# GNN megakernel on one core: the setup around a power on GpSimd, with operands and results moved to PSUM, the power cut in two, and the step masks made later

## What is computed

```python
def reference(x, src, dst, edge_attr, edge_weight, edge_weight1, ...):
    h = layernorm_relu(x)                                   # "norm_x"
    ew = concat([edge_weight, ones(N)])                     # edges and loops
    deg = segment_sum(ew, dst_and_loops, N)
    dis = where(deg > 0, rsqrt(deg), 0)
    for W, b in ((W0, b0), (W1, b1), (W2, b2)):             # three GCN layers
        h = relu(segment_sum((h @ W)[src] * dis[src] * ew * dis[dst], dst) + b)
    ...                                                     # a GIN layer: segment_sum(ew * x[src])
    att = edge_weight1 ** lam                               # the power; used only in the attention
    ...                                                     # attention over the edges: segment softmax, masks by node
    ...                                                     # a SAGE layer: a mean over the in-edges
```

## Time and profile before

| | us |
|---|---|
| median of 3 runs | 6796.12 |
| the profiled execution | 6801.79 |
| its span | 6800.1 |
| GpSimd busy, of the span | 4779.3 (70%) |
| VectorE busy | 3946.1 (58%) |
| TensorE busy | 4822.0 (71%) |
| ScalarE busy | 1132.7 (17%) |
| first gather of pass 0 starts | 305.0 |

### The profile page before, as it was taken

One profiled execution on the slowest core, in us unless ns is written; L12 is line 12 of the kernel. 1 busy time (PEld: TensorE's weight loads), 2 busy tenths in 40 slices (PEclk: granted clock), 3 DMA queues, 4 the chain that ended last, 5 costly groups with the idle time before them and its releaser, 6 DMA issues.

```text
span 6800.1 us, 95655 instructions
## 1 busy us (share of the span) xinstructions
PE 4822.0 (71%) x25896; PEld 3192.9 (47%) x25896; DVE 3946.1 (58%) x11854; ACT 1132.7 (17%) x2990; POOL 4779.3 (70%) x4783
## 2 busy tenths in 40 slices
PE   0367667677767677777577777699999974777775
PEld 0244444444444444444344444566666653444444
DVE  8744555544555545555544444588888886444445
ACT  0200000100000100000100000377777763000000
POOL 6377777777777677777677777477777742777773
PEclk9788998888898888888788888899999987888887
DMA  2122222222222222222222222366666641222221
GB/s 56 47 53 53 53 54 53 72 53 53 53 53 53 67 53 53 53 53 53 61 53 53 53 53 53 82 141 143 142 146 140 142 94 32 53 53 53 53 53 47
DMA packets 384863, 466.43 MB, mean 69 GB/s; under 512 B 103802, under 2 KB 290616, under 8 KB 384326
## 3 DMA queue, kind: packets, MB, share of 16 engines
q0 software_dynamic: 152528, 313.83, 18.6%
q1 hardware_dynamic: 201066, 129.25, 8.4%
q10 hardware_dynamic: 30748, 17.23, 0.9%
HBM read 434.51 MB, written 27.81 MB: 68 GB/s over the span
## 4 chain that ended last, share of the span: by engine, by line
POOL 46%; issue 19%; PE 13%; DVE 10%; DMA 9%; SPq 2%; ACT 1%; DVEq 1%; ACTq 0%; POOLq 0%
POOL pool L710 45%; DMA pool<-table,src_col 4%; DMA pool<-edge_attr 3%; DVE work L1538 2%; PE psum L896 2%; PE psum L887 2%; PE psum L880 2%; PE psum L850 2%; PE psum L922 1%; DMA gath<-table,src_col 1%; DVE pool L1380 1%; PE psum L824 1%; SPq L611 1%; PE psum L848 1%; PE psum L866 1%
## 5 line engine op out<-in xcount | busy, mean ns | idle before, releaser
L710 POOL DMA_INDIRECT pool<-table,src_col x3910 | 3701.1, 947 | 1467.1 <-issue 1143.8
L850 PE MATMUL psum<-pool 128*128 x8300 | 1924.0, 321 | 1413.0 <-DVE pool L1546 1409.7
L850 PEld LDWEIGHTS psum<-pool 128*128 128x128 f32 x8300 | 1695.8, 220 | 2556.1 <-issue 2231.9
L848 PE MATMUL psum<-busy_rows,iota_b 128*128 128x512 bf16 x7820 | 2694.1, 431 | 72.3 <-issue 72.1
L1546 DVE TENSOR_SCALAR pool<-iota_f,rel_col,ew_col 128x128 f32<-128x128 f32 x3320 | 1225.3, 370 | 1803.7 <-SPq L492 1789.2
L690 POOL DMA_INDIRECT gath<-table,src_col x832 | 904.6, 1087 | 281.4 <-issue 223.9
L1538 DVE SCALAR_TENSOR_TENSOR work<-psum,dis,work 128x128 f32 x2490 | 870.9, 350 | 144.2 <-PE psum L850 112.8
L848 PEld LDWEIGHTS psum<-busy_rows,iota_b 128*128 128x128 bf16 x7820 | 847.6, 110 | 181.7 <-issue 95.9
L1546 DVE TENSOR_SCALAR pool<-iota_f,rel_col 128x128 f32<-128x128 f32 x830 | 267.6, 323 | 436.8 <-SPq L492 433.3
L1081 ACT ACTIVATE pool<-psum 128x512 f32<-128x512 f32 (+1 forms) x104 | 58.1, 565 | 1989.4 <-PE psum L812 1989.4
L1538 DVE SCALAR_TENSOR_TENSOR work<-psum,inv_cnt,work 128x128 f32 x830 | 291.4, 351 | 106.2 <-PE psum L850 76.9
(11 more groups left out here) (212 smaller groups left out, 3767.9 us busy)
## 6 DMA issues: line engine op xcount, KB each, us to landing
pool<-table,src_col POOLq DMA_INDIRECT x3910
pool<-edge_attr SPq DMA_DIRECT2D x832, 64.0 KB
pool<-step_masks SPq DMA_DIRECT2D x624, 48.0 KB
pool<-rel_rows SPq DMA_DIRECT2D x208, 128.0 KB
gath<-table,src_col POOLq DMA_INDIRECT x832
table<-work ACTq DMA_DIRECT2D x48, 256.0 KB, 2.3
table<-QV SPq DMA_DIRECT2D x12, 256.0 KB, 2.3
table<-work SPq DMA_DIRECT2D x12, 256.0 KB, 2.3
```

What stands on the lines that cost most here:

```text
L710: gp.indirect_dma_start(out=gath_ring[:, t % RING, :], out_offset=None, in_=source[:, :], in_offset=bass.IndirectOffsetOnAxis(ap=src_col[: ...
L848: pe.matmul(psum[:, SUM_BANKS, :], iota_b[:, :], busy_rows[:, :], start=True, stop=True)
L850: pe.matmul(psum[:, steps.bank(s), 0:D], hot_ring[:, s % HOT_RING, :], gath_ring[:, bass.ds(slots[s % REGS], 1), :].rearrange("p a d -> p ...
```

## The change

1. **The power.** `lam` and the distances are loaded first of all, on ScalarE's queue (they were late on ScalarE's and SyncE's). VectorE makes `lam_row` ahead of the plan. GpSimd computes the first 100 of 800 elements (`FIRST_POW`) before the seven indirect DMAs and the other 700 right behind them, without the wait for `norm_x.shift`.
2. **PSUM operands.** The ones exist in SBUF and in PSUM (`ones_col`, `ones_ps`), and an instruction takes the one on the other side of its tensor. Destinations (`dst_ps`), digits, `block2`, `rstd_ps`, the low digit (`low_ps`) and the weights (`ew_ps`, the transposed weights left in their banks) are in PSUM. `tile_src` is cast in two halves of 7 x 64, in place, straight. The low digit's instructions are halved.
3. **The right-hand side of the degrees** is made by four instructions per chunk, one for each digit, instead of from a one-hot `low_hot` made ahead.
4. **Order.** Only six of the ten blocks of columns (destinations, weights, sources) are turned before the degrees. All the rest of the masks, with the other four, is `masks_vector`, behind the last `gcn_drain(0)`. ScalarE stores the rows of each group as before, but scales `AGG` for all 13 groups only after `masks_made`. The waits of the gathers for `src_kept` and of `dis` for `masks_stored` are gone from there; ScalarE waits for both behind the scaling. In the masks, instructions with a second input of ones are `tensor_scalar` or `tensor_copy` now.

The diff, cut to its core:

```diff
@@ gpsimd
+            gp.wait_ge(lam_made, 1)
+            gp.tensor_tensor(dist_sb[:, 0:FIRST_POW], dist_sb[:, 0:FIRST_POW], lam_row[:, 0:FIRST_POW],
+                             ALU.pow).then_inc(pow_made, 1)
             gp.wait_ge(tile_idx_made, 1)
...
-            gp.wait_ge(lam_made, 1)
-            gp.wait_ge(dist_loaded, 16)
-            gp.wait_ge(norm_x.shift, NGR)
-            gp.tensor_tensor(dist_sb, dist_sb, lam_row, ALU.pow).then_inc(pow_made, 1)
+            gp.tensor_tensor(dist_sb[:, FIRST_POW:DC], dist_sb[:, FIRST_POW:DC], lam_row[:, FIRST_POW:DC],
+                             ALU.pow).then_inc(pow_made, 1)
             gathers(gp, 0, table[0], passes[0])
@@ gathers
             gp.wait_ge(stored[which], 16 * NGR)
-            if which == 0:
-                gp.wait_ge(src_kept, 32)
@@ tensor
-            pe.wait_ge(masks_made, 1)
-            for n, (arr, dest, lo, hi) in enumerate(COLS):
...
+            pe.wait_ge(rel_made, 1)
+            turn_columns(pe, 0, EARLY)
...
-            dense(pe, gcn[0], [AGG], ["W0"], lambda g: pe.wait_ge(norm_x.normed, norm_x.before + g + 1))
+            dense(pe, gcn[0], [Y], ["W0"], lambda g: pe.wait_ge(norm_x.normed, norm_x.before + g + 1))
+            pe.wait_ge(masks_made, 1)
+            turn_columns(pe, EARLY, len(COLS))
@@ scalar
+            dense_copies(act, gcn[0], 1, ACT.Copy, first_keep)
+            act.wait_ge(masks_made, 1)
+            for g in range(NGR):
+                gcn_start(g)
+            act.wait_ge(masks_stored, 48)
+            act.wait_ge(src_kept, 32)
@@ vector
+            settle()
+            v.wait_ge(dist_loaded, 32)
+            v.tensor_scalar(lam_row, lam_row, lam_col[0:DR, 0:1], None, ALU.add).then_inc(lam_made, 1)
             plan_vector(v, own, settle)
-            v.wait_ge(weights_loaded, WEIGHTS_LOADED)
-            v.tensor_scalar(lam_row, lam_row, lam_col[0:DR, 0:1], None, ALU.add).then_inc(lam_made, 1)
...
             for g in range(NGR):
                 gcn_drain(0, g)
+            masks_vector(v, own, settle)
@@ step_rows_vector
+            for lo in range(0, SR, GROUP):
+                hi = min(SR, lo + GROUP)
+                v.tensor_copy(dst_ps[:, lo:hi, :], raw_field[:, lo:hi, DST, :]).then_inc(own.up(), 1)
+            v.wait_ge(src_loaded, 48)
+            for lo in range(0, P, P // 2):
+                v.tensor_copy(tile_src[:, :, lo:lo + P // 2], tile_src_i[:, :, lo:lo + P // 2]).then_inc(own.up(), 1)
+            settle()
+            for lo in range(0, SR, GROUP):
+                hi = min(SR, lo + GROUP)
+                ins = v.tensor_tensor(rel[:, lo:hi, :], dst_ps[:, lo:hi, :],
+                                      spread(base_of[:, lo:hi].rearrange("p (s a) -> p s a", a=1), 2, P), ALU.subtract)
+            ins.then_inc(rel_made, 1)
+            take_columns(v, 0, EARLY)
@@ degrees_vector
-            v.scalar_tensor_tensor(low, rel_ij, float(HIGH), const(ONE, low), ALU.is_ge, ALU.mult).then_inc(own.up(), 1)
+            for low_h, lo, hi in halves:
+                v.scalar_tensor_tensor(low_h, rel_ij[:, lo:hi, :], float(HIGH), ones(ones_ps, low_h), ALU.is_ge,
+                                       ALU.mult).then_inc(own.up(), 1)
...
-            v.tensor_tensor(low_hot, spread(flat_low, 2, LOW), spread(iota_f[:, 0:LOW].rearrange("p (a l) -> p a l", a=1), 1, NS),
-                            ALU.is_equal).then_inc(own.up(), 1)
...
                 v.tensor_tensor(hot_2[:, k % 2, :, :], spread(flat_high[:, lo:hi, :], 2, HIGH),
-                                spread(iota_f[:, 0:HIGH].rearrange("p (a h) -> p a h", a=1), 1, CHUNK),
-                                ALU.is_equal)
-                here = rhs[:, k % 2, :, :, :]
-                v.tensor_tensor(here, spread(parts[:, lo:hi, :].rearrange("p s (k a) -> p s k a", a=1), 3, LOW),
-                                spread(low_hot[:, lo:hi, :].rearrange("p s (a l) -> p s a l", a=1), 2, PARTS),
-                                ALU.mult).then_inc(deg_hot, 1)
+                                spread(digits.rearrange("p (a h) -> p a h", a=1), 1, CHUNK), ALU.is_equal)
+                of_chunk = spread(low_ps[:, 2 * k // CHUNKS, lo % (NS // 2):lo % (NS // 2) + CHUNK].rearrange(
+                    "p (s a) -> p s a", a=1), 2, PARTS)
+                for digit in range(LOW):
+                    ins = v.scalar_tensor_tensor(rhs[:, k % 2, :, :, digit], of_chunk, float(digit), parts[:, lo:hi, :],
+                                                 ALU.is_equal, ALU.mult)
+                ins.then_inc(deg_hot, 1)
...
-            v.wait_ge(masks_stored, 48)
-            v.scalar_tensor_tensor(dis[:, :], deg[:, :], 0.0, dis[:, :], ALU.is_gt, ALU.mult).then_inc(dis_made, 1)
+            v.scalar_tensor_tensor(dis[:, :], psum[:, 4, 0:NB], -1.0, dis[:, :], ALU.is_gt, ALU.mult).then_inc(dis_made, 1)
```

More of the change, by code:

```diff
@@ L223, in build @@
         block_hot = pool[:, 3 * SRW:3 * SRW + 8 * NB].rearrange("p (m b) -> p m b", m=8)
-        low_hot = pool[:, 0:NS * LOW // 2].bitcast(BF16).rearrange("p (s l) -> p s l", l=LOW)
-        rest, low, high = (pool[:, k * SRW:k * SRW + NS].rearrange("p (i j) -> p i j", j=QUADS) for k in (5, 6, 8))
+        high = pool[:, 8 * SRW:8 * SRW + NS].rearrange("p (i j) -> p i j", j=QUADS)
         def by_quarter(col):
@@ L794, in tensor, with turn_columns @@
             products(pe, passes[4], dense_stages(pe, sage_dense, [AGG, Y], ["Wl", "Wr"], complete(passes[4])))
+        def turn_columns(pe, first, end):
+            for n in range(first, end):
+                arr, dest, lo, hi = COLS[n]
+                if n >= first + 4:
+                    pe.wait_ge(cols_made, n - 3)
+                for i in range(lo, hi):
+                    ins = pe.transpose(psum[:, n % 4, (i - lo) * P:(i - lo + 1) * P], arr[:, i, :], ident[:, :])
+                ins.then_inc(cols_turned, 1)
         def dense(pe, d, sources, names, given):
@@ L984, in gcn_start, with first_keep @@
                 ins.then_inc(gcn_started, 1)
-            for layer in range(3):
+            def first_keep(g):
+                if g >= 1:
+                    gcn_keep(0, g - 1)
+                if g == NGR - 1:
+                    gcn_keep(0, g)
+            dense_copies(act, gcn[0], 1, ACT.Copy, first_keep)
[4 more added lines that the diff above has]
+            act.wait_ge(src_kept, 32)
+            for layer in range(1, 3):
                 def start(g, layer=layer):
                     if g >= 1:
-                        gcn_start(layer, g - 1)
+                        gcn_keep(layer, g - 1)
+                        gcn_start(g - 1)
                     if g == NGR - 1:
-                        gcn_start(layer, g)
-                dense_copies(act, gcn[layer], 1, ACT.Copy if layer == 0 else ACT.Relu, start,
-                             bias=gcn_bias[:, layer - 1:layer] if layer else 0.0)
+                        gcn_keep(layer, g)
+                        gcn_start(g)
+                dense_copies(act, gcn[layer], 1, ACT.Relu, start, bias=gcn_bias[:, layer - 1:layer])
             def keep_gin(g):
@@ L1359, in norm_x_vector, with take_columns @@
             settle()
-            v.scalar_tensor_tensor(ln_rstd[:, :], ln_mv[:, :, 1], LN_EPS, const(ONE, ln_rstd[:, :]), ALU.add,
+            v.scalar_tensor_tensor(ln_mv[:, :, 1], ln_mv[:, :, 1], LN_EPS, ones(ones_ps, ln_rstd[:, :]), ALU.add,
                                    ALU.mult).then_inc(norm_x.var, NGR)
             v.wait_ge(norm_x.root, NGR)
-            v.reciprocal(ln_rstd[:, :], ln_rstd[:, :]).then_inc(own.up(), 1)
+            v.reciprocal(rstd_ps, ln_mv[:, :, 1]).then_inc(own.up(), 1)
             settle()
-            v.scalar_tensor_tensor(ln_shift[:, :], ln_mv[:, :, 0], -1.0, ln_rstd[:, :], ALU.mult,
-                                   ALU.mult).then_inc(norm_x.shift, NGR)
+            move(v, ln_rstd[:, :], rstd_ps).then_inc(own.up(), 1)
+            v.scalar_tensor_tensor(ln_shift[:, :], ln_mv[:, :, 0], -1.0, rstd_ps, ALU.mult, ALU.mult).then_inc(norm_x.shift, NGR)
         def move(v, dest, source):
-            return v.scalar_tensor_tensor(dest, source, 1.0, const(ONE, dest), ALU.mult, ALU.mult)
+            return v.scalar_tensor_tensor(dest, source, 1.0, ones(ones_col, dest), ALU.mult, ALU.mult)
+        def take_columns(v, first, end):
+            for n in range(first, end):
+                arr, dest, lo, hi = COLS[n]
+                v.wait_ge(cols_turned, n + 1)
+                move(v, dest[:, lo * P:hi * P], psum[:, n % 4, 0:(hi - lo) * P]).then_inc(cols_made, 1)
         def step_rows_vector(v, own, settle):
```

146 lines of the change are left out of this document (77 added, 69 removed).

## The result

The changed kernel takes 6850.2 us (median of 4 runs, 6842.0 to 6860.3) against 6798.5 (median of 4, 6792.8 to 6807.2): a ratio of 1.0076, 95% interval 1.0057 to 1.0094. It is about 52 us slower. The forecast, 6796 us and at most 6807, was wrong.

A forecast was written before the change was run, and what follows sets the result against it. GpSimd's gathers were taken to set the pace, so only pass 0's start counted: tile 16 at 325.2 us against 325.06, +0.1 on the profiled 6801.79, or 6796 us on the median; range 6676 to 6807.

The forecast's parts named there:

- what moves it moves the end one for one: Any shift of pass 0's seventeenth gather was claimed to shift the kernel's end by the same amount.
- The mark: Start of pass 0's seventeenth gather (tile 16, first needing a free slot): forecast at 325.2 us against 325.06 before.
- Its pieces: GpSimd's power in two parts: 100 elements in 16.0 us, 700 in 112.1 us, from 64.0 to 176.1.
- the cost of the loads on the plan: Delay from moving the `lam` and distance loads to the queue's head: taken as 0, bounds 0 to 16.6 us.
- The wait of the cast: VectorE's in-place half casts of `tile_src`, reached at about 72.6 us, were claimed to wait for the power's end, 176.1.
- The first rival: The half casts do not wait, so VectorE's chain runs 103.5 us earlier: 6693 us, or 6677 with fast writes; chance 0.32.
- a chunk: One of eight steps making the degrees' right-hand side: forecast 3.54 + 3.95 = 7.49 us, 59.9 for all eight.
- the drains: Dense layer without scaling of `AGG`: drains 1.33 us apart, ending 18.2 us behind `dis` instead of 20.9.
- Rivals 2 and 3: Digit instructions at one element per cycle (6781 us, chance 0.17), or slower than any row, over 1.41 us (6816, 0.05).
- the columns and digits ahead of them: VectorE's work between power and chunks (casts, copied columns, digits, weights): forecast from 176.1 to 197.9 us.
- 37 us are released: Remark that VectorE's released 37 us go into slower chunks (17), a stall (13.4) and the rest of the power wait.
- The stall at tile 16: GpSimd waiting at pass 0's seventeenth gather because masks now stand unhidden before pass 0: forecast 13.4 us.

The follow-up runs named there:

- e2: Kernel before with only its power split into two pieces of 400 elements, both in the old place: 7946.3 us, ratio 0.9893.
- c3: Changed kernel with one-piece power behind the indirect DMAs, `lam` and distance loads last on ScalarE's queue, `tile_src` cast with two inputs, one in PSUM: 6707.6 us.
- c1: Changed kernel with both pieces of the power (100 and 700 elements) behind the seven indirect DMAs: 6710.6 us, ratio 0.9865.
- e1: Changed kernel with two power pieces of 400 behind the indirect DMAs, `lam` and distance loads last on ScalarE's queue, `lam` added behind the plan: 7929.6 us, ratio 0.9871.
- a1: Changed kernel with the power in one piece of 800 elements behind the seven indirect DMAs: 6828.2 us, ratio 1.0027.
- b1: Kernel before with only `lam` and distances loaded first, `lam` added ahead of the plan, and the power split as in the change: 6840.1 us, ratio 1.0039.
- d3: c3 with a power of 128 x 8 scratch elements on GpSimd ahead of the first indirect DMA: 6748.0 us, ratio 0.992.
- a2: Changed kernel with an unused 32-byte tile that puts the gathers' buffers back at their earlier addresses: 6849.7 us, ratio 1.0062.
- c2: Changed kernel with one GpSimd memset of 128 x 8 between the power's second piece and the first gather: 6836.2 us, ratio 1.0049.
- d4: c3 with a multiplication of 128 x 8 scratch elements on GpSimd ahead of the first indirect DMA: 6714.3 us, ratio 0.987.
- e3: Changed kernel with a GpSimd memset and scratch multiplication between the power's second piece and the gathers: 8029.7 us (one run), where the kernel before takes 8032.8.

## Why the prediction was wrong

**The step that failed** is in the first paragraph: "The change touches no pass, so its whole worth is how much earlier the gathers of pass 0 run", and "what moves it moves the end one for one". The mark was right, and where the gathers keep their pace the rule holds to some 9 us: in e2 86.2 us at the mark and 86.5 at the end; in c3 103.6 (325.06 less 221.50) and 94.7 by the medians, 97.9 by the spans; in c1 97.5 and 91.7; in e1 109.7 and 103.2. What failed is the condition. The change places a power ahead of the first indirect DMA, and each gather of the first four passes takes 11 ns more, 34 us in all: shown from both sides by a1 and c1 (taken away), b1 and d3 (put in). The remainder of the 52, some 18 us, is not explained by one cause. In the two profiles attention was 26 us longer. At most some 9 of these are the slow gathers again (832 of about 10 ns, an estimate from their medians); a2 (8 us) and c2 (3 us) show most of the rest to be scatter. The same changed kernel with an unused tile added (a2) is 38 us over its before, and with a memset (c2) 34. These three measurements of one change, 34, 38 and 52 us, are as near as its own loss is known.

**The power.** Its pieces were sized right (16.4 and 112.2, forecast 16.0 and 112.1). Set at nothing was the cost of the loads on the plan, with lateness of the two loads as its bound. The loads were early enough: the first piece started at 9.93 and was over at 26.31, ahead of the plan. But the plan itself started at 28.07, 4.7 later, still waiting for its own load, <-DMA pool<-dst. c3, d3 and e1, with the two loads behind, start at 22.1 to 23.1; b1, which only moved the loads and the power, at 28.01. Of a moved DMA I had counted when it lands, not whose landing it delays. The second piece ended at 180.3 in place of 176.1.

**The wait of the cast** was forecast and came: the halves end 0.6 behind the power. The Trainium skill's rule (VectorE: DVE Perf Modes, "What auto-detection actually checks"), 7 against 7 counts as equal and so works two at a time, is borne out: free of the power, 448 elements take 412 ns, less than half of the 1.08 us that 896 took one at a time. But rows like L1403 could not tell that this wait hangs on the length of the power. Beside 400 elements the same instruction, and L1380 with its two inputs, run free. The first rival, which needed no wait, had 6693; its mechanism was dismissed on a row of a power of 800, and one statement of the change set elsewhere (both pieces behind the DMAs) makes it true, at 6711.

**Chunks, digits and drains.** L1508's four take 3.85 us, forecast 3.95; a chunk 7.2 for 7.49; the drains 1.33 apart as expected. Rivals 2 and 3, with 0.5 and over 1.41 for a digit instruction, are refuted by about 0.96. The eight chunks gave 2.3 us back, and the columns and digits ahead of them 2.1 (they start 19.7 behind the power's end, forecast 21.8). With the power 4.2 later, `dis` still ended on the forecast's time: errors that cancel (271.4 for 271.0), and to that extent the right mark was luck. The remark behind the sum that 37 us are released does not follow from its terms, which give 30.4 (23.5 of the power's end, 4.2 of columns and digits, 2.7 of the drains) against 17.2 for the chunks and 13.4 at tile 16; the forecast does not rest on it.

**The stall at tile 16** was forecast at 13.4 and is 9.85: the gathers beside the masks take longer, the seventh 1.82 us, which makes 2.3 of the difference, and the mark came 1.2 earlier than forecast.

## What to carry to other kernels

Ask of a moved operation not only what waits for it but what it leaves behind on its engine: on GpSimd the order of a power and the first indirect DMA set the pace of thousands of gathers. Compare medians of a repeated instruction by stage, since a few ns each are lost in a mean. Where a long GpSimd operation shuts VectorE out, try it in shorter pieces first; here that one-line edit to the kernel before gave 86.5 us, where the whole restaging lost about 50. Both pieces of 400 behind the DMAs with the loads last (e1) gave 103 us on its chip, against 86.5 for that edit in the same group.

## What was not expected of the hardware

- After a `tensor_tensor` power on GpSimd ahead of the first indirect DMA, the median gather takes 955 or 958 ns instead of 944 or 947 (means 955 to 962 and 944 to 950). A power of 128 x 8 elements does it (d3), a multiplication there does not (d4). It lasts through attention's gathers (1008 against 999) and is over in the last pass. In e3, one execution, the gathers behind a multiplication were normal (947); a memset did not do it (956). Why is open: no run shows what happens inside GpSimd.
- VectorE's fast cast and its two-input instruction wait for a GpSimd power of 700 or 800 elements; neither waits for one of 400, and the cast not for one of 100. Between 400 and 700 nothing was tried. The Trainium skill (SBUF — State Buffer, "SBUF: two separate sides") has the shared pair of ports held for the whole instruction by whichever comes first; with 700 elements the cast's wait agrees (104.26 us, to the end), with 400 it does not (0.7), and in the earlier trace rows L1380 was let go 45 us before the power's end. The measurements decide. The two-input instruction was let go 83 us after the start of the power and not at a time that depends on its end: 154.8 less 71.5 with 800 elements, and 158.65 less 75.59 with 700 (b1, below). The casts that started later, 93.6 us into the power before and 93.4 in b1, were held to its end. No run shows why.
- The other way round VectorE can hold up the power: 84.2 us for 400 elements beside a dense chain of SBUF instructions, 64.3 for the half behind it (e2, one execution).
- Two loads placed at the head of ScalarE's queue delay what waits for SyncE's load of `dst` by nearly 5 us: 28.07 against 23.32 before and 22.1 to 23.1 in c3, d3 and e1. SyncE's issue of that load takes 20.56 us after and 13.82 before.

GpSimd's and VectorE's rows of b1 for the second point:

```profile
75.59 112.17 POOL L663 TENSOR_TENSOR QV<-QV 125x700 f32<-125x700 f32 x1 [7.47 <-DVE ln_shift L1368]
79.51 79.14 DVE L1383 TENSOR_TENSOR pool<-pool,base_of 128x896 f32<-128x896 f32 x1
168.97 19.62 DVE L1406 CAST work<-work 128x896 f32<-128x896 int32 x1
```
